# A fused attention and expert layer on one core: the first norm one sequence ahead, the output projection in round 9, and new places for the small pieces

## The reference, cut to what matters

```
h   = layernorm(x)                                  # "first norm", gives xn
Q, K, V = h @ W_q + b_q, h @ W_k + b_k, h @ W_v + b_v        # 16 heads of 8
scores = (Q K^T + relative-position term) / sqrt(8), causal
out = softmax(scores) @ V + relative-position term of V
x1  = x + layernorm(out @ W_o + b_o)                # "second norm"
f   = layernorm(x1)                                 # "third norm"
x2  = x1 + layernorm(shared_expert(f) + top-2 of 8 routed experts(f))
```

## Time and profile before

| | |
|---|---|
| median of 3 runs | 1033.69 us (1032.93 to 1034.54) |
| the profiled execution's own time | 1030.79 us |
| its span in the profile | 1029.1 us |
| attention phase (19 steps) | up to about 720 us of the span |
| length of steps 3 to 15 | 40.1 to 42.8 us |
| mean granted clock of PE | 0.939 |
| busy: PE, DVE, POOL, ACT | 898.8, 817.6, 728.0, 680.5 us |

### The profile page before, as it was taken

One profiled execution on the slowest core, in us unless ns is written; L12 is line 12 of the kernel. 1 busy time (PEld: TensorE's weight loads), 2 busy tenths in 40 slices (PEclk: granted clock), 3 DMA queues, 4 the chain that ended last, 5 costly groups with the idle time before them and its releaser, 6 DMA issues. The chain is left out here.

```text
span 1029.1 us, 25739 instructions
## 1 busy us (share of the span) xinstructions
PE 898.8 (87%) x8935; PEld 526.4 (51%) x8935; DVE 817.6 (79%) x1948; ACT 680.5 (66%) x1315; POOL 728.0 (71%) x946
## 2 busy tenths in 40 slices
PE   2888988999899988998999898887679999999995
PEld 0443444544445444444444444433357777777773
DVE  4787888888888888887888888876667888878884
ACT  3247777767668777776777867665346767676773
POOL 5244686686776867768668777566257989898886
PEclk9999999989889999898899998987889999999998
DMA  3311111111111111111111111001425454545541
GB/s 82 137 34 26 29 43 28 35 46 27 29 27 38 43 28 33 40 27 35 28 36 46 28 31 37 25 26 43 162 62 156 150 170 153 164 150 166 163 138 31
DMA packets 58828, 70.88 MB, mean 69 GB/s; under 512 B 8944, under 2 KB 34416, under 8 KB 58720
## 3 DMA queue, kind: packets, MB, share of 16 engines
q1 hardware_dynamic: 56432, 69.04, 23.1%
q10 hardware_dynamic: 2288, 0.42, 0.2%
HBM read 43.75 MB, written 8.65 MB: 51 GB/s over the span
## 5 line engine op out<-in xcount | busy, mean ns | idle before, releaser
L1137 DVE TENSOR_REDUCE mx<-ps_s 128x1 f32<-128x512 f32 (+2 forms) x640 | 410.2, 682 | 75.2 <-PE ps_s L1549 74.2
L809 ACT ACTIVATE prob<-ps_e 128x512 f32<-128x512 f32 x640 | 352.0, 608 | 110.3 <-PE ps_e L1506 110.2
L651 POOL TENSOR_SCALAR_AFFINE_SELECT prob<-prob 128x516 f32<-128x516 f32 (+1 forms) x320 | 176.6, 576 | 150.2 <-ACT prob L809 150.1
L1530 PE MATMUL ps_s<-ks,qs 31*128 31x512 f16 (+3 forms) x1024 | 196.5, 324 | 32.2 <-DVE mx L1137 27.0
L1572 PE MATMUL ps_av<-prob,vp 128*32 128x512 f32 (+3 forms) x2048 | 202.5, 495 | 4.3 <-POOL prob L651 4.2
L731 POOL TENSOR_TENSOR hidden_low<-hidden,hidden_high 128x512 fp32r<-128x512 f32 x144 | 191.0, 1354 | 12.0 <-ACT hidden_high L998 10.7
L1506 PE MATMUL ps_e<-qs,ks 32*128 32x512 f16 (+3 forms) x1024 | 167.9, 316 | 6.2 <-ACT prob L809 2.0
L1530 PEld LDWEIGHTS ps_s<-ks,qs 31*128 31x128 f16 x1024 | 54.9, 94 | 167.6 <-issue 89.4
L1549 PE MATMUL ps_s<-masked_at,below 32*128 32x64 bf16 (+3 forms) x2560 | 135.0, 192 | 0.0
L998 ACT CAST hidden_high<-hidden 128x512 fp32r<-128x512 f32 x160 | 98.0, 613 | 30.7 <-DVE hidden L1450 27.5
L1549 PEld LDWEIGHTS ps_s<-masked_at,below 32*128 32x128 bf16 x2560 | 105.6, 98 | 20.0 <-issue 4.1
(11 more groups left out here) (173 smaller groups left out, 1664.3 us busy)
## 6 DMA issues: line engine op xcount, KB each, us to landing
gate_rows<-gates_dram SPq DMA_DIRECT2D x128, 256.0 KB, 3.7
qs<-qh SPq DMA_DIRECT2D x64, 64.0 KB, 2.1
xnT_dram<-oT SPq DMA_DIRECT2D x16, 256.0 KB, 2.0
xeT<-xnT_dram SPq DMA_DIRECT2D x16, 256.0 KB, 2.8
out<-result SPq DMA_DIRECT2D x16, 256.0 KB, 2.3
v_near<-v_back SPq DMA_DIRECT2D x16, 254.0 KB
ks<-kh SPq DMA_DIRECT2D x62, 64.0 KB, 2.1
qs<-ql SPq DMA_DIRECT2D x32, 64.0 KB, 2.1
```

The lines of the kernel that those rows point to most:

```text
L651: pool.affine_select(out=v, in_=v, compare_op=ALU.is_ge, fill=0.0, base=-2, pattern=cols, channel_multiplier=-1).then_inc(S["p_masked"], 1)
L809: act.activation(prob[g % 2][:, u, b, :], ps_e[bank][:, :], ACT.Exp, scale=SCALE).then_inc(S["e_done"], 1)
L1137: dve.tensor_reduce(out, src, AX.X, ALU.max).then_inc(s_free[bank], 1)
L1530: pe.matmul(scores[:, at:at + P * (qt + 1)], qs[par][rows, pr, P * qt:P * qt + P], ks[par][rows, pr, 0:P * (qt + 1)], start=(n == 0), stop ...
```

## The change

The first norm of sequence t+1 is computed in step t on POOL, after the split of Q and K; its statistics are taken on DVE in step t too (for sequence 1, at the end of step 0). The transpose xT is then the first piece of its step (round 0 in place of 6), q goes to round 3 (from 9) and k to 5 (from 10). Since V of a sequence is computed one step after its xT, there are now two xnT buffers, used in turn. v0 goes to round 8 (from 5), oproj to 9 (from 11), s_tok to 10 (from 7). The calls on ACT, POOL and DVE move with them. The load of x has a semaphore more: sequences 1 and 2 are loaded at the start one by one, the other 13 later together. The amount of computation is the same.

```diff
-AT = {"e_sums": 1, "av2": 2, "m1": 4, "v0": 5, "av3": 6, "xT": 6, "s_tok": 7, "oT": 7, "q": 9,
-      "k": 10, "oproj": 11, "av0": 14, "m0": 15, "av1": 17, "xn2": 18, "logits": 19}
+AT = {"xT": 0, "e_sums": 1, "q": 3, "m1": 4, "k": 5, "oT": 7, "v0": 8, "oproj": 9, "s_tok": 10,
+      "av2": 2, "av3": 6, "av0": 14, "m0": 15, "av1": 17, "xn2": 18, "logits": 19}
...
-            xnT = sb_front("xnT", [P, 1 + SEQ])
+            xnT0 = sb_front("xnT0", [P, 1 + SEQ])
...
-            sb_attention("apart", [P, 2 * NPAIR, SEQ], F16)
+            xnT1 = sb_attention("xnT1", [P, 1 + SEQ])
+            sb_attention("apart", [P, 2 * NPAIR * SEQ - 2 * (1 + SEQ)], F16)
...
-            sp.dma_start(xr[:, 1, :]...x_v[:, 1]).then_inc(x_loaded[1], 16)
+            for s in (1, 2):
+                sp.dma_start(xr[:, s, :]...x_v[:, s]).then_inc(x_loaded[s], 16)
...
 POOL, step
+                if st.t0 == 0:
+                    norm1(0)
                 if st.B:
                     near_half(st, st.b, 1)
-                masks(0, 3)
-                if st.F:
-                    normalise(st, st.f, xn[:, :, :], ...)
-                masks(3, 10)
+                masks(0, 5)
                 if st.F:
                     split(st)
+                    if st.f + 1 < NSEQ:
+                        norm1(st.f + 1)
                 if st.t0 == 0:
                     masked_columns()
-                masks(10, 12)
+                masks(5, 10)
                 if st.C:
                     second norm, addition to x
-                masks(12, 15)
+                masks(10, 15)
                 if st.C:
                     third norm
-                masks(15, 16)
                 if st.F:
                     near_products(st)
-                masks(16, 20)
+                masks(15, 20)
...
 ACT, step, after (the calls of before stand in the kernel above)
+                xT_out
+                exps(0, 2)   s_rows_out   exps(2, 3)   p_near_exp(b, 1)
+                exps(3, 6)   q_out
+                exps(6, 8)   mT_out(b, 1)   exps(8, 9)   av_out(c, 3)
+                exps(9, 10)  k_out
+                exps(10, 13) kd_out(0)   exps(13, 14)   oT_out
+                exps(14, 16) v_out
+                exps(16, 20) av_out(b, 0)   kd_out(1)
+                exps(20, 31) ...   exps(35, 36)   xn2T_out
+                exps(36, 38) logits_out   exps(38, 39) av_out(b, 2)   exps(39, 40)
...
 DVE, step, after
+                ln1_bn of the next sequence   maxima(0, 2)   max_half(b, 1)   maxima(2, 3)   av_tok_out(c, 2)
+                maxima(3, 7)   aggregate of the first norm   maxima(7, 11)   av_tok_out(c, 3)
+                maxima(11, 16) values_out                 (before: after maxima(9, 10))
+                maxima(16, 18) y_out, y_bn                (before: after maxima(18, 22))
+                maxima(18, 19) aggregate of the second norm
+                maxima(19, 22) s_tok_out                  (before: after maxima(13, 18))
+                maxima(22, 24) max_half(a, 0)   maxima(24, 28) av_tok_out(b, 0)
+                maxima(28, 29) x1_bn                      (before: after maxima(28, 30))
+                maxima(29, 31) aggregate of the third norm (before: after maxima(30, 32))
+                maxima(31, 36) av_tok_out(b, 1)   maxima(36, 40)
```

More of the change, by code:

```diff
@@ L46 @@
 PROB_AT = {(pr, kt): (u, at) for u, parts in enumerate(E_UNITS) for pr, kt, at in parts}
-AT = {"e_sums": 1, "av2": 2, "m1": 4, "v0": 5, "av3": 6, "xT": 6, "s_tok": 7, "oT": 7, "q": 9,
-      "k": 10, "oproj": 11, "av0": 14, "m0": 15, "av1": 17, "xn2": 18, "logits": 19}
-STAGE = {"av2": "C", "e_sums": "A", "m1": "B", "s_tok": "A", "av3": "C", "v0": "A", "oT": "C", "xT": "F",
-         "oproj": "C", "q": "F", "k": "F", "av0": "B", "m0": "A", "av1": "B", "xn2": "C", "logits": "C"}
+AT = {"xT": 0, "e_sums": 1, "q": 3, "m1": 4, "k": 5, "oT": 7, "v0": 8, "oproj": 9, "s_tok": 10,
+      "av2": 2, "av3": 6, "av0": 14, "m0": 15, "av1": 17, "xn2": 18, "logits": 19}
+STAGE = {"e_sums": "A", "m1": "B", "s_tok": "A", "av2": "C", "av3": "C", "v0": "A", "oT": "C", "xT": "F",
+         "oproj": "C", "q": "F", "k": "F", "m0": "A", "av0": "B", "av1": "B", "xn2": "C", "logits": "C"}
 STAGE.update({f"s{i}": "A" for i in range(NUNIT)})
@@ L208, in end @@
     def end(self):
-        if LOOP0 <= self.st.t0 < NSEQ and self.per_step != self.n - self.first:
+        if LOOP0 <= self.st.t0 < NSEQ - 1 and self.per_step != self.n - self.first:
             raise AssertionError((self.n - self.first, self.per_step))
@@ L365, in block_kernel @@
             qs, ks = [qs0, qs1], [ks0, ks1]
+            xnT = [xnT0, xnT1]
         w_first = sb("w_first", [P, 12, P])
@@ L404, in block_kernel @@
         S = {n: sem(n) for n in names}
-        x_loaded = [S["x_loaded0"], S["x_loaded1"], S["x_loaded2"]]
+        x_loaded = [S[f"x_loaded{i}"] for i in range(4)]
         stacks = [[S[f"stacks{par}{half}"] for half in range(2)] for par in range(2)]
@@ L816, in xT_out @@
                 act.wait_ge(S["e_full"], n + 1)
-                act.copy(xnT[:, 1:1 + SEQ], ps_e[bank][:, :]).then_inc(S["e_done"], 1)
+                act.copy(xnT[st.f % 2][:, 1:1 + SEQ], ps_e[bank][:, :]).then_inc(S["e_done"], 1)
             def q_out(st):
@@ L934, in step @@
                     p_near_exp(st, st.b, 1)
-                exps(3, 7)
+                exps(3, 6)
+                if st.F:
+                    q_out(st)
+                exps(6, 8)
                 if st.B:
                     mT_out(st, st.b, 1)
-                exps(7, 9)
+                exps(8, 9)
                 if st.C:
                     av_out(st, st.c, 3)
+                exps(9, 10)
+                if st.F:
+                    k_out(st)
+                exps(10, 13)
+                if st.F:
+                    kd_out(st, 0)
+                exps(13, 14)
+                if st.C:
+                    oT_out(st)
+                exps(14, 16)
                 if st.A:
                     v_out(st)
[L943 to L952, removed]
+                exps(16, 20)
                 if st.B:
@@ L1311, in step @@
                 maxima(3, 7)
-                if st.F:
+                if after:
                     aggregate(st1, mv1, "stats1")
-                maxima(7, 9)
-                maxima(9, 10)
-                if st.A:
-                    values_out(st)
-                maxima(10, 11)
+                maxima(7, 11)
                 if st.t0 == NSEQ + 2:
@@ L1330, in step @@
                     gates_second(0, EARLY)
-                maxima(13, 18)
+                maxima(13, 16)
                 if st.A:
-                    s_tok_out(st)
-                maxima(18, 22)
+                    values_out(st)
+                maxima(16, 18)
                 if st.C:
@@ L1604, in values @@
                 for i in range(NT):
-                    last = pe.matmul(u[:, i * P:i * P + P], xnT[:, 1 + i * P:1 + i * P + P], wv[:, :],
+                    last = pe.matmul(u[:, i * P:i * P + P], xnT[st.a % 2][:, 1 + i * P:1 + i * P + P], wv[:, :],
                                      start=True, stop=True)
```

80 lines of the change are left out of this document (44 added, 36 removed).

## The result

The changed kernel takes 1068.3 us (median of four runs, 1066.2 to 1072.6), the kernel before 1033.6 beside it: ratio 1.034, 95% interval 1.0306 to 1.0375. It is 34.7 us slower. The forecast was 1045, range 1015 to 1057: the direction is right, the size is not.

The account below looks back on a forecast made before the run. No engine is full; waits passed between engines set a step. Parts of 19.0 + 15.0 + 7.0 = 41.0 us against 40.14 give 11.2 over 13 steps, plus 0.4 at the start: 11.6 on 1033.7 is 1045 us, range 1015 to 1057.

Parts of the forecast that it names:

- The wait for xn: PE's wait for the first norm, 1.2 us a step, which the change was to remove.
- From R0 to values_out, 19.0: First part of a full-clock step, to the start of DVE's values_out: 19.0 us, bound by ACT's gapless 7.9 us chain.
- R0: The start of round 0 of a step, from which the forecast counts its times.
- e13: The exponential on ACT that ends its gapless 7.9 us chain from q_out, forecast to end at R0 + 15.5.
- the first rival: Between q's issue and v0, ACT's pieces overlap better and the run is faster: 1006 us, half of it 1020; chance 0.27.
- From values_out to the third statistics, 15.0: Second part, on DVE: 22.8 us before, less 2.44 of waits, 4.3 of units and 1.1 of av3, leaves 15.0.
- From there on, 7.0: Last part: POOL's third norm, its transpose, logits and last round until the next step, unchanged at 7.0 us.
- The sum: The three parts of a full-clock step, 19.0 + 15.0 + 7.0 = 41.0 us, against 40.14 before: 0.86 longer.
- The clock, 1.35 a step, kept: Step time lost to the lowered clock, 1.35 us a step, claimed unchanged because PE's work and busy share hardly change.
- xT in round 0, 0.2 a step: PE's delay in round 0, its next scores waiting for ACT to free a ring place: 0.2 us, bounds 0.2 and 0.7.
- oproj two rounds earlier: On DVE, the 0.58 us wait for the addition to x goes and the third norm's statistics come one 0.61 unit earlier.
- The start: At the kernel's start POOL computes sequence 1's norm ahead of masked_at: 0.4 us longer, between 0 and 2.

Follow-up runs that it names:

- after_xT1: The changed kernel with xT in round 1 in place of 0, its read on ScalarE one exponential later: 1069.0 us.
- after_k10: The changed kernel with k put back to round 10 and POOL's split after the masks of round 9; q stays in round 3: 1074.1 us.
- norm_ahead: The kernel before with only the first norm one sequence ahead and two xnT buffers, all other places old: 1025.0 us.
- na_oproj9: The kernel before with the first norm one sequence ahead, and oproj in round 9 with y_out, second norm and x1_bn moved along: 1012.2 us.

## Why the prediction was wrong, and where it was right

- **The wait for xn goes, and the time is not simply gained.** Right; the norm ahead alone is worth 9 us of the 15.6.
- **From R0 to values_out, 19.0.** Measured 19.67, and 18.9 with the stretched instructions away. Of the 0.67 too much, 0.34 have come by the start of q (R0 + 6.84 for 6.5, inside the bounds of that term), the rest behind e13. The number was nearly right, by luck, and its reason was not: ACT's chain is as long as forecast (7.8 us for 7.9, without a gap), but kd_out moved out of it changes nothing. The sentence that PE's own work would allow R0 + 16 is the mistaken one: PE has 18.34 us of work in that stretch. With it falls the way in which the first rival, the faster one, could have come true.
- **From values_out to the third statistics, 15.0.** Measured 16.31. This is the step that failed in the sum: the pieces of DVE were taken with their durations of before, where `d` runs beside the short start of POOL's second norm. The change puts max_half beside the addition to x, and `d` takes 1.75 us for 0.29. The units and waits that the forecast took out did go: with the split later, `d` takes 0.29 again and the part is 14.86, all of the computation kept.
- **From there on, 7.0.** Measured 7.13, with 0.46 of idle time of PE ahead of xn2, not near 1. It is ended by DVE (`num`, 143.41), not by POOL's norm (143.20): av_tok_out must first read the bank that xn2 takes.
- **The sum.** 41.0 forecast, 43.1 measured at full clock; 13 x 2.1 = 27 us is the miss, and 1045 + 27 is 1072, close to the 1068.3 measured. Of the 2.1, 1.3 belong to the second part and its `d`, 0.7 to the first, 0.1 to the third.
- **The clock, 1.35 a step, kept.** Right for this kernel (1.2), by luck rather than by argument: in kernels that differ from it by one place or two the mean clock over the same steps is between 0.877 and 0.938. The rule of the Trainium skill quoted in the prediction ("TensorE: Matmul & The Clock Gate", section "A second HAM failure mode: psum-queue depth-cycling") named a real danger, a clock that swings, but not this kernel's time. Whether idle times bring the fall is not shown: their sum does not order the kernels (PE is idle for 6.0 us a step in after_xT1, at a mean clock of 0.938, and for 5.1 in after_k10, at 0.877).
- **xT in round 0, 0.2 a step.** Too low: about 1 at equal clock and a lower clock beside it, in both pairs that tell it apart (POOL's norm moves with it in both).
- **oproj two rounds earlier.** Priced as a wait of 0.58 and one unit of 0.61, so 1.2 a step or 15 us; alone it is worth 12.8, of which 0.7 a step show at full clock.
- **The start.** 0.4 forecast, 1.6 measured at the first e_sums (26.1 to 27.7), inside its bounds. PE's first long wait ends 0.4 later (24.70 to 25.13), as forecast; most of the rest is xT, which now stands ahead of them.
- **The signs named for right and wrong.** Nearly all of those for "right" came: values_out at R0 + 19.67, 4.4 us of waits for scores on DVE in rounds 3 to 8, ACT without a gap up to e13, x1_bn without its wait. Only the length at full clock, 43.1 for 41, and the wait for xn2 did not. Such signs say where the pieces stand, not what binds; that took an edit.

Open is what makes the 1.7 us or more a step that early q and k cost at equal clock beyond the stretch, and why the clock settles where it does in each variant. No kernel was tried in which the clock is held while one place moves.

## What to carry to other kernels

When work is moved between places, a duration read from the old trace holds only if its neighbours on the other engines stay the same: look at what runs beside each instruction in its new place, above all VectorE instructions with two SBUF operands beside GpSimd's. Split a change of many places into its places and time them one by one: here a gain of 26 us (norm, oproj, s_tok) was buried under a loss of 61. And where the granted clock moves, a step shorter at equal clock is not yet a shorter run; compare both.

## What the hardware showed that was not expected

- Two VectorE instructions of 128x32 elements took 1.75 us in place of 0.29 beside a GpSimd addition of 1.28 us and the mask behind it; `d` went from 270 to 668 ns in the mean, `o_tok` from 664 to 938. Beside a GpSimd instruction of 128x4 elements (1.01 us) `d` kept 184 to 193 ns each. One-operand reductions in their place took 181 and 420.
- The clock can take back what a step gains. 2.9 us of VectorE's work less a step made a step at 0.96 two us shorter (42.0 to 42.3 against 43.9 to 44.4) and the run only 4 us; the mean clock fell from 0.926 to 0.904. With the split later, 1.45 us gained in one part came back as a clock of 0.80 in the next. It is no rule: from norm_ahead to na_oproj9 steps became shorter and the clock rose, 0.937 to 0.957.
- Steps settle at one length: the changed kernel with max_half later, the split later or xT in round 1 has five or more steps of 44.3 to 44.4 us at 0.92, and the changed kernel itself two, while their busy time on DVE differs by up to 1.8 us.
- Moves of one piece by one to six rounds changed the whole by -13 to +32 us.
